# Attention over 16 images: one stream of steps across all batches, with the projections spread between them and every low part of the probabilities on GpSimd

## The chip, the core and the metric

The kernel runs on one core of one Trainium2 chip. TensorE (PE; its weight loads are the row PEld), VectorE (DVE), ScalarE (ACT) and GpSimd (POOL) compute, and SyncE (SP) issues the transfers. The metric is the device time of one execution in microseconds, as the median of several runs.

## What is computed

Each of 16 images is a batch of N = 1024 tokens with 512 channels, in float32, and goes through one attention layer of 8 heads of 64 dimensions:

```
qkv  = x @ w_qkv + b_qkv
qkv  = qkv.reshape(B, N, 8, 192)
q, k, v = jnp.split(qkv, 3, axis=-1)
attn = jnp.einsum('bxhd,byhd->bxyh', q, k) * 64 ** -0.5
attn = jax.nn.softmax(attn, axis=2)
res  = jnp.einsum('bxyh,byhd->bxhd', attn, v).reshape(B, N, 512)
out  = res @ w_out + b_out + x
```

## The kernel before

Float32 accuracy is kept with split operands. A number is the sum of a high part (rounded to fp32r, or to f16 for the probabilities P and for v) and a low part (what the rounding left), and a product is the sum of hi·hi, hi·lo and lo·hi. So a projection over 512 channels is 4 × 3 = 12 matmuls (`TERMS`), each with a 128 × 128 stationary operand and 512 moving columns.

**Fills.** Four kinds of work fill a PSUM bank for another engine to empty. `x_transpose` and `o_transpose` are four 128 × 128 transposes of a tile of 128 tokens (of x, or of the heads' output). `qk` (a head, half of the tokens), `v` (a tile of tokens, all heads) and `project` (a tile of tokens) are 12 matmuls each (line 472). ScalarE writes the high part (`xT_hi`, `v_parts`, `q_hi_hi`, `k_lo_hi`; lines 616 to 633), VectorE the low part (`xT_lo`, `v_parts`, `k_lo_hi`, `q_shift`; lines 712 to 728), and for `project` VectorE adds the sum to `y_tile` (line 736). SP copies q and k to the other 64 partitions once their high parts are there.

**Steps.** A unit is a head and half of its queries (16 units), and has 4 steps of 2 key tiles each, 64 steps a batch. TensorE computes the scores of a step (lines 532 and 534, two matmuls a tile), ScalarE takes the exponential of both tiles twice, as float32 `p_full` and as f16 `p_hi` (lines 654 and 655), VectorE or GpSimd subtracts them to get the low part `p_lo` (line 771 or 380, by `POOL_STEPS`), and TensorE multiplies with v in 24 small matmuls (lines 556 to 560, `step_pv`). The maximum of each row is found before: 8 matmuls a unit (line 503), each reduced by VectorE (line 749), joined, transposed (line 510) and put into `q_shift` (line 762), so that the scores come out with the maximum subtracted.

**Order.** Every engine has its program written out in order for one batch, and a loop over 16 batches runs it. A batch is a list `BEFORE` (8 x-transposes, the first 4 `v`, the first `qk`), then slots -5 to 65, then a list `AFTER`. In slot s TensorE issues the early row maxima, the scores of step s + 1, a piece of `qk` for the next head, the late row maxima, and P·V of step s - 1. The loop starts the next batch behind the last projection. PSUM has eight banks: four for scores, two in turn for row maxima, one for P·V, one for fills in the steps. Waits are on counting semaphores; TensorE and the other engines each take their instructions in order.

Of the kernel before, what the change touches and what calls it, by code (L numbers as in the profile page):

```python
# [19 lines left out]
Q_TILES = HALF // P  # L20
UNITS = HEADS * HALVES
STEPS_PER_UNIT = 4
STEPS = UNITS * STEPS_PER_UNIT
KEYS_PER_STEP = TOKENS // STEPS_PER_UNIT // P
X_SLOTS, Y_SLOTS, P_SLOTS = 4, 4, 3
SCORE_BANKS = (0, 1, 2, 3)
FILL_BANK_STEADY = 7
PV_BANK = 6
V_WIDTH = 2 * DIM + 2
PV_W = DIM + 1  # L30
FIRST_SLOT = -5
LAST_SLOT = STEPS + 1

MAX_TILES = (((0, 1), (2,)), ((3, 4), ()), ((5, 6), (7,)), ((), ()))
MAX_TILES_OF_UNIT = {0: (((0, 1), ()), ((2, 3), ()), ((4, 5), ()), ((6, 7), ())),
                     1: (((0, 1), ()), ((2, 3), ()), ((4, 5), (6,)), ((7,), ()))}


def max_tiles_of_slot(s, late=False):

    unit, slot = divmod(s + 5, STEPS_PER_UNIT)
    if not 0 <= unit < UNITS:  # L50
        return []
    tiles = MAX_TILES_OF_UNIT.get(unit, MAX_TILES)
    return [("row_max", unit, n // 2, n % 2) for n in tiles[slot][late]]


def shift_unit_of_slot(s):

    unit, rest = divmod(s + 2, Q_TILES)
    return unit if rest == 0 and 0 <= unit < UNITS else None


TERMS = 3 * CH_TILES


QK_PARTS = ({-5: (0, 1), -4: (1, 4), -3: (4, 8), -2: (8, TERMS)}, {0: (0, 6), 1: (6, TERMS)})
V_OF_SLOT = {-5: (4,), -4: (5,), -3: (6,), -2: (7,)}


def fills_of_slot(s):


    parts = [(("v", t), 0, TERMS) for t in V_OF_SLOT.get(s, ())]
    for h in range(1, HEADS):
        begin = 8 * (h - 1)
        for half in range(2):
            if s - begin in QK_PARTS[half]:
                parts.append((("qk", h, half), *QK_PARTS[half][s - begin]))
    tail = {STEPS - 2: (("o_transpose", 0), ("o_transpose", 1)),
            STEPS - 1: (("project", 0), ("o_transpose", 2)),
            STEPS: (("project", 1), ("o_transpose", 3), ("project", 2))}  # L80
    return parts + [(w, 0, TERMS) for w in tail.get(s, ())]


def completed_in_slot(s):

    return [w for w, _, last in fills_of_slot(s) if last == TERMS]


def is_first_half(w):
    return w[0] == "qk" and w[2] == 0  # L90


def consumed_in_slot(s):


    return ([w for w in completed_in_slot(s - 1) if is_first_half(w)]
            + [w for w in completed_in_slot(s) if not is_first_half(w)])


def high_parts_in_slot(s):  # L100


    parts = [(w, "k") for w in completed_in_slot(s - 1) if is_first_half(w)]
    for w in completed_in_slot(s):
        parts.append((w, "q" if is_first_half(w) else "qk"))
    return parts


def named(*names):

    kinds = {"T": ("x_transpose",), "V": ("v",), "Q": ("qk", 0)}
    return [(*kinds[name[0]], int(name[1])) for name in names]

BEFORE = named("T0", "T1", "T2", "T3", "V0", "T4", "T5", "Q0", "T6", "T7", "V1", "V2", "Q1", "V3")
AFTER = [("o_transpose", 4), ("project", 3), ("o_transpose", 5), ("project", 4), ("o_transpose", 6),
         ("project", 5), ("o_transpose", 7), ("project", 6), ("project", 7)]
SLOTS = range(FIRST_SLOT, LAST_SLOT + 1)

MAX_ORDER = []
for _s in SLOTS:
    MAX_ORDER += max_tiles_of_slot(_s) + max_tiles_of_slot(_s, late=True)
    if shift_unit_of_slot(_s) is not None:
        MAX_ORDER.append(("shift", shift_unit_of_slot(_s)))
MAX_AT = {w: n for n, w in enumerate(MAX_ORDER)}
MAXES = len(MAX_ORDER)

FILL_ORDER = BEFORE + [w for _s in SLOTS for w, _, last in fills_of_slot(_s) if last == TERMS] + AFTER
FILL_AT = {w: n for n, w in enumerate(FILL_ORDER)}  # L130
FILLS = len(FILL_ORDER)
assert FILL_ORDER == BEFORE + [w for _s in SLOTS for w in consumed_in_slot(_s)] + AFTER
HI_ORDER = [w for w in FILL_ORDER if w[0] != "project"]
HI_AT = {w: n for n, w in enumerate(HI_ORDER)}
HIS = len(HI_ORDER)


def fill_banks():


    banks, after = {}, 0
    for n, w in enumerate(FILL_ORDER):
# [12 lines left out]
FILL_BANK = fill_banks()


def last_in_bank(w):

    before = [u for u in FILL_ORDER[:FILL_AT[w]] if FILL_BANK[u] == FILL_BANK[w]]  # L160
    return before[-1] if before else None

POOL_STEPS = (0, 2, 3, 4, 6, 7)
LAST_UNIT_POOL_STEPS = (STEPS - 4, STEPS - 2)


def on_pool(s):  # L170
# [12 lines left out]

def signals(batch, per_batch, n):

    return batch * per_batch + n


def signals_led(batch, per_batch, n):

    return batch * per_batch + n + 1


def attention_block(nc: bass.Bass, x, w_qkv, b_qkv, w_out, b_out, out):
# [7 lines left out]
    with ExitStack() as ctx:  # L202
# [6 lines left out]

# [5 lines left out]
        xT_lo = sb("xT_lo", [P, CH_TILES, TOKENS], f32r)  # L215
        x_in = sb("x_in", [P, X_SLOTS, CH], f32)
# [7 lines left out]
        p_hi = sb("p_hi", [P, P_SLOTS, KEYS_PER_STEP, HALF], f16)  # L224
        p_lo = sb("p_lo", [P, P_SLOTS, KEYS_PER_STEP, HALF], f16)
# [15 lines left out]


# [593 lines left out]
```

## Time and profile before

| | |
|---|---|
| median of 3 runs | 4104.45 us (4103.89 to 4105.86) |
| the profiled execution | 4103.61 us, its span 4101.8 us |
| TensorE busy | 3915.1 us, 38156 matmuls |
| VectorE, ScalarE busy | 2721.0 us, 2707.0 us |
| GpSimd busy | 1769.3 us |
| granted TensorE clock | 1.00 of 2.4 GHz |

The span runs from the first to the last instruction. Matmuls overlap in the records, so TensorE's busy time says less than the distance from the start of one matmul to the start of the next.

### The profile page before, as it was taken

Reading aid. Unit: us, or ns where it says so; the run is one execution under the profiler, and the core shown is the slowest. Engines: PE = TensorE matmul, PEld = TensorE weight load, DVE = VectorE, ACT = ScalarE, POOL = GpSimd, SP = SyncE. Lnnn points to the kernel's source line nnn. Section 1 sums busy time; section 2 is a strip of 40 time slices with the busy share of each in tenths; the row PEclk is TensorE's granted clock in tenths of the full one; section 3 lists DMA queues with packets and bytes.
Section 4 is the critical chain, followed back from the end, with each engine's and each line's share of the span. In section 5 each row is a group of like instructions: output and inputs, shape, how many; then the busy total and the mean of one; then the engine's idle time right before and its main releaser. Section 6 shows DMA issues by size and latency. Waiting matters only on the chain.

```text
span 4101.8 us, 105442 instructions
## 1 busy us (share of the span) xinstructions
PE 3915.1 (95%) x38156; PEld 3113.8 (76%) x38156; DVE 2721.0 (66%) x4395; ACT 2707.0 (66%) x2965; POOL 1769.3 (43%) x888
## 2 busy tenths in 40 slices
PE   6999999999999999999999999999999999999999
PEld 5777777777777777777777777777777777777777
DVE  5757757577575775757667576675766757667576
ACT  4756847568475774757757477574775747657476
POOL 1534525345253552535525255352553525435254
PEclk9999999999999999999999999999999999999999
DMA  3011021110202102020021211202011121110201
GB/s 98 22 54 42 20 76 25 57 39 17 79 22 70 26 20 76 22 74 22 25 71 24 71 24 28 68 22 73 22 37 58 25 71 25 38 58 22 63 22 43
DMA packets 100845, 179.85 MB, mean 44 GB/s; under 512 B 16192, under 2 KB 16192, under 8 KB 100288
## 3 DMA queue, kind: packets, MB, share of 16 engines
q1 hardware_dynamic: 100288, 172.29, 14.9%
q8 instruction: 366, 6.00, 0.6%
q14 instruction: 191, 1.56, 0.1%
HBM read 71.57 MB, written 33.55 MB: 26 GB/s over the span
## 4 chain that ended last, share of the span: by engine, by line
PE 68%; DVE 17%; issue 11%; ACT 1%; DVEq 1%; POOL 1%; DMA 0%; SPq 0%; ACTq 0%; POOLq 0%
PE psum L472 31%; PE psum L503 9%; PE psum L532 6%; PE psum L534 6%; DVE max_parts L749 6%; PE psum L556 4%; PE psum L560 4%; PE psum L558 4%; DVE q_shift L728 3%; DVE k_lo_hi L726 3%; DVE p_lo L771 2%; PE psum L486 2%; DVE q_shift L762 2%; ACT p_hi L655 1%; POOL p_lo L380 1%
## 5 line engine op out<-in xcount | busy, mean ns | idle before, releaser
L380 POOL TENSOR_TENSOR p_lo<-p_full,p_hi 128x1024 f16<-128x1024 f32 x752 | 1607.3, 2143 | 2069.7 <-ACT p_hi L655 2069.7
L749 DVE TENSOR_REDUCE max_parts<-psum 128x1 f32<-128x512 f32 x2048 | 1341.3, 686 | 516.7 <-PE psum L503 507.8
L654 ACT ACTIVATE p_full<-psum,prob_bias 128x1024 f32<-128x1024 f32 x1024 | 1144.1, 1117 | 384.8 <-PE psum L534 371.1
L655 ACT ACTIVATE p_hi<-psum,prob_bias 128x1024 f16<-128x1024 f32 x1024 | 1137.2, 1111 | 0.0
L556 PEld LDWEIGHTS psum<-v_parts,p_hi 128*128 128x128 f16 x8192 | 743.8, 98 | 263.2 <-issue 161.8
L556 PE MATMUL psum<-v_parts,p_hi 128*128 128x65 f16 x8192 | 857.2, 193 | 35.5 <-DVE o_heads L781 19.9
L558 PE MATMUL psum<-v_parts,p_hi 128*128 128x64 f16 x8192 | 850.7, 192 | 0.0
L560 PE MATMUL psum<-v_parts,p_lo 128*128 128x65 f16 x8192 | 848.0, 194 | 0.0
L532 PE MATMUL psum<-q_hi_hi,k_lo_hi 128*128 128x512 f32 x2048 | 818.7, 400 | 1.9
L503 PE MATMUL psum<-k_lo_hi,q_hi_hi 128*128 128x512 f32 x2048 | 769.3, 429 | 51.7 <-DVE q_shift L728 21.5
L534 PE MATMUL psum<-q_shift,k_shift 128*128 128x512 f32 x2048 | 802.3, 392 | 0.0
L558 PEld LDWEIGHTS psum<-v_parts,p_hi 128*128 128x128 f16 x8192 | 753.9, 97 | 2.5
L560 PEld LDWEIGHTS psum<-v_parts,p_lo 128*128 128x128 f16 x8192 | 754.2, 97 | 0.0
L503 PEld LDWEIGHTS psum<-k_lo_hi,q_hi_hi 128*128 128x128 f32 x2048 | 367.3, 189 | 158.9 <-DVE q_shift L762 60.3
L534 PEld LDWEIGHTS psum<-q_shift,k_shift 128*128 128x128 f32 x2048 | 385.1, 188 | 73.4
L532 PEld LDWEIGHTS psum<-q_hi_hi,k_lo_hi 128*128 128x128 f32 x2048 | 385.0, 188 | 70.7 <-issue 3.8
L472 PE MATMUL psum<-xT_hi,wqkv_hi 128*128 128x512 f32 x1024 | 414.6, 405 | 11.6
L472 PE MATMUL psum<-xT_hi,wqkv_lo 128*128 128x512 f32 x1024 | 408.8, 399 | 0.0
L472 PE MATMUL psum<-xT_lo,wqkv_hi 128*128 128x512 f32 x1024 | 401.6, 392 | 0.0
L616 ACT CAST xT_hi<-psum 128x512 fp32r<-128x512 f32 x256 | 141.0, 593 | 367.3 <-PE psum L486 366.9
L625 ACT ACTIVATE q_hi_hi<-psum,qk_bias 64x512 fp32r<-64x512 f32 x256 | 174.3, 681 | 279.4 <-PE psum L472 279.4
L771 DVE TENSOR_TENSOR p_lo<-p_full,p_hi 128x1024 f16<-128x1024 f32 x272 | 332.2, 1221 | 31.1 <-ACT p_hi L655 31.1
(61 smaller groups left out, 4269.8 us busy)
## 6 DMA issues: line engine op xcount, KB each, us to landing
x_in<-in_x SPq DMA_DIRECT2D x128, 256.0 KB, 3.9
k_shift<-k_lo_hi SPq DMA_DIRECT2D x256, 128.0 KB, 2.2
q_hi_hi<-q_hi_hi SPq DMA_DIRECT2D x256, 128.0 KB, 2.3
y_tile<-in_x SPq DMA_DIRECT2D x128, 256.0 KB, 2.8
result<-y_tile SPq DMA_DIRECT2D x128, 256.0 KB, 2.8
o_heads<-in_L_conv_w_qkv SPq DMA_DIRECT2D x12, 256.0 KB, 4.1
o_heads<-in_L_conv_w_out SPq DMA_DIRECT2D x4, 256.0 KB, 4.1
out_bias<-in_L_conv_b_out SPq DMA_DIRECT2D x1, 256.0 KB, 5.8
```

Of the source, the lines that this page charges most:

```text
L380: nc.gpsimd.tensor_tensor(p_lo[:, s % P_SLOTS, :, :], p_full[:, s % 2, :, :], p_hi[:, s % P_SLOTS, :, :], ALU.subtract).then_inc(p_lo_read ...
L472: matmul = nc.tensor.matmul(fill_bank(w), a, b, start=n == 0, stop=n == TERMS - 1)
L503: nc.tensor.matmul(dst, q_hi_hi[:, h % 2, q0:q0 + P], k_lo_hi[:, h % 2, k_half * HALF:(k_half + 1) * HALF], start=True, stop=True).then_in ...
L532: nc.tensor.matmul(score_banks(s)[:, n, :], k_lo_hi[:, h % 2, keys], q_hi_hi[:, h % 2, cols], start=True, stop=False)
L534: last = nc.tensor.matmul(score_banks(s)[:, n, :], k_shift[:, h % 2, keys], q_shift[:, h % 2, cols], start=False, stop=True)
L556: nc.tensor.matmul(pv[:, qt, :], hi, v_parts[:, kt, h, DIM:DIM + PV_W], start=kt == 0 and qt == 0, stop=False, skip_group_check=True)
L558: nc.tensor.matmul(pv[:, qt, 0:DIM], hi, v_parts[:, kt, h, 0:DIM], start=False, stop=False, skip_group_check=True)
L560: last = nc.tensor.matmul(pv[:, qt, :], lo, v_parts[:, kt, h, DIM:DIM + PV_W], start=False, stop=kt == TOKEN_TILES - 1, skip_group_check=True)
L654: nc.scalar.activation(p_full[:, s % 2, :, :], score_banks(s), ACT.Exp, scale=SCALE, bias=prob_bias[:, :])
L655: nc.scalar.activation(p_hi[:, s % P_SLOTS, :, :], score_banks(s), ACT.Exp, scale=SCALE, bias=prob_bias[:, :]).then_inc(exp_done, 1)
L749: nc.vector.reduce_max(max_parts[:, u % 2, q_tile, k_half:k_half + 1], max_bank(w), AX.X).then_inc(max_tile_done, 1)
L771: nc.vector.tensor_tensor(p_lo[:, s % P_SLOTS, :, :], p_full[:, s % 2, :, :], p_hi[:, s % P_SLOTS, :, :], ALU.subtract).then_inc(p_lo_read ...
```

## The change

The loop's body is no longer a batch. All batches form one stream of steps, 64 a batch, and the fills of a batch are put at fixed slots relative to its step 0, from -17 to 103, so that they lie between steps of the batch before or after. Each engine's program is a first part (slots -17 to 45), a loop over 15 times 64 slots in which two batches meet, and a last part; SP's is written out whole. A table gives each fill its slot:

- x-transposes, the first half of `v` and the first `qk` stand in slots -17 to -1, that is in slots 47 to 63 of the batch before. `v` is now made in two groups of 4 heads, with 256 columns instead of 512, the second in slots 11 to 31.
- o-transposes stand in slots 62 to 72 and projections in 66 to 103, which are slots 2 to 39 of the next batch. They write to tiles of their own (`oT_hi`, `oT_lo`, 3 slots).
- In each slot TensorE does early row maxima, transposes, pieces of `qk`, `v` or `project`, scores, late row maxima, P·V. Slots 19, 27, 34, 42, 43 and 44 have no fill.
- Scores use three banks in turn (four before), and each of the two tiles of a step has its own signal and its own pair of exponentials of 512 columns (one pair of 1024 before). Two banks serve the fills, and two the row maxima.
- All of `p_lo` is made by GpSimd (6 of 8 steps before, 2 of 4 in the last unit). `p_hi` has 4 slots and `p_lo` 2 (3 each before); x tiles have 2 slots (4 before), y tiles 3 (4 before).
- Each kind of work has its own semaphores.

```diff
-STEPS_PER_UNIT = 4
-X_SLOTS, Y_SLOTS, P_SLOTS = 4, 4, 3
-SCORE_BANKS = (0, 1, 2, 3)
-FILL_BANK_STEADY = 7
...
+X_SLOTS, Y_SLOTS, O_SLOTS, HI_SLOTS, LO_SLOTS = 2, 3, 3, 4, 2
+V_GROUP = HEADS // 2
...
+SCORE_BANKS, PV_BANK, RING_BANKS, FILL_BANKS = (0, 1, 2), 6, (4, 5), (3, 7)
...
+FIRST_SLOT, LAST_SLOT = -17, STEPS + 39
+LOOP_SLOT = 46
+
+X_TRANSPOSE_SLOT = (-17, -16, -15, -13, -12, -12, -11, -10)
+O_TRANSPOSE_SLOT = (62, 64, 65, 67, 68, 69, 70, 72)
+PROJECT_PARTS = (((66, 0, TERMS),), ((67, 0, TERMS),), ((68, 0, TERMS),), ((69, 0, TERMS),), ((71, 0, TERMS),),
+                 ((74, 0, 6), (76, 6, TERMS)), ((99, 0, 6), (100, 6, TERMS)), ((103, 0, TERMS),))
+V_SLOT = ((-14, -13, -9, -6, -5, -4, -3, -1), (11, 15, 18, 20, 23, 26, 28, 31))
+Y_BIAS_SLOT = (54, 56, 58, 67, 69, 71, 73, 76)
...
+def qk_parts(h, half):
+
+
+    begin = 8 * (h - 1)
+    if half == 1:
+        return [(begin, 0, 6), (begin + 1, 6, TERMS)]
+    if h == 2:
+        return [(begin - 2, 0, TERMS)]
+    return [(begin - 3, 0, 4), (begin - 2, 4, TERMS)]
...
-POOL_STEPS = (0, 2, 3, 4, 6, 7)
-LAST_UNIT_POOL_STEPS = (STEPS - 4, STEPS - 2)
...
+POOL_STEPS = tuple(range(8))
...
+def slots(batches):
+
+    return {"first": [(c, (0,)) for c in range(FIRST_SLOT, LOOP_SLOT)],
+            "loop": [(c, (0, 1)) for c in range(LOOP_SLOT, LOOP_SLOT + STEPS)],
+            "last": [(c, (0,)) for c in range(LOOP_SLOT, LAST_SLOT + 3)]}[batches]
...
+            def exp_tile(i, g, n):
+                s = g % STEPS
+                if n == 0:
+                    if g >= 2 or not isinstance(i, int):
+                        wait_low(act, i, g - 2)
+                    wait_for(act, pv_done, i, STEPS, g + 1 - HI_SLOTS)
+                wait_for(act, scores_ready, i, SCORE_TILES, KEYS_PER_STEP * g + n + 1)
+                nc.scalar.activation(p_full[:, s % 2, n, :], scores(s, n), ACT.Exp, scale=SCALE, bias=prob_bias[:, :])
+                nc.scalar.activation(p_hi[:, s % HI_SLOTS, n, :], scores(s, n), ACT.Exp,
+                                     scale=SCALE, bias=prob_bias[:, :]).then_inc(exp_done, 1)
```

**VectorE, the end of a batch before,** as the instructions stand in its program: projections (`y_tile`) and o-transposes (`xT_lo`) follow each other with nothing between them.

```order
L736 TENSOR_TENSOR y_tile<-psum,y_tile 128x512 [waits y_biased]
L739 REGISTER_ALU
L710 REGISTER_ALU [waits fill_ready]
L712 TENSOR_TENSOR xT_lo<-psum,xT_hi 128x4x128 [waits hi_done]
L739 REGISTER_ALU
L734 REGISTER_ALU [waits fill_ready]
L736 TENSOR_TENSOR y_tile<-psum,y_tile 128x512 [waits y_biased]
```

**VectorE, the same work after the change,** in slots 2 and 3 of the next batch (`oT_lo` is the low part of an o-transpose):

```order
L746 TENSOR_REDUCE row_max<-max_parts 128x4 [waits row_max_done]
L726 SCALAR_TENSOR_TENSOR k_lo_hi<-psum,qk_bias,k_lo_hi 64x512 [waits qk_hi_done]
L728 SCALAR_TENSOR_TENSOR q_shift<-psum,qk_bias,q_hi_hi 64x512
L752 TENSOR_TENSOR q_shift<-psum,minus_block 4x512 [waits shift_ready]
L737 TENSOR_TENSOR y_tile<-psum,y_tile 128x512 [waits project_ready,y_biased]
L199 REGISTER_ALU
L742 TENSOR_REDUCE max_parts<-psum 128x1 [waits row_max_ready]
L199 REGISTER_ALU
L710 TENSOR_TENSOR oT_lo<-psum,oT_hi 128x512 [waits o_transpose_hi_done]
L199 REGISTER_ALU
L742 TENSOR_REDUCE max_parts<-psum 128x1 [waits row_max_ready]
L737 TENSOR_TENSOR y_tile<-psum,y_tile 128x512 [waits project_ready,y_biased]
```

The projection's addition now stands behind the low parts of q and k and the shift, and between row maxima.

**VectorE, a step in the middle of a head before,** with the low part of the probabilities between the output of a unit and a row maximum:

```order
L777 RECIPROCAL inv_sum<-psum 128x4 [waits pv_done]
L781 TENSOR_TENSOR o_heads<-psum,inv_sum 128x4x64 [waits inv_ready]
L769 REGISTER_ALU
L770 REGISTER_ALU [waits exp_done]
L771 TENSOR_TENSOR p_lo<-p_full,p_hi 128x1024 [waits pv_done]
L745 REGISTER_ALU
L749 TENSOR_REDUCE max_parts<-psum 128x1 [waits max_tile_ready]
```

After the change the row maximum follows the output directly; no p_lo is left in VectorE's program.

```order
L774 RECIPROCAL inv_sum<-psum 128x4 [waits o_ready,pv_done]
L777 TENSOR_TENSOR o_heads<-psum,inv_sum 128x4x64 [waits inv_ready]
L199 REGISTER_ALU
L742 TENSOR_REDUCE max_parts<-psum 128x1 [waits row_max_ready]
```

**TensorE after the change, slots 42 and 43,** which have no fill (line 504 is a row maximum, 512 the transpose for the shift, 536 and 538 scores, 558 the first of the 24 matmuls of P·V, left out here):

```order
L504 MATMUL psum<-k_lo_hi,q_hi_hi 128x512 [waits q_hi_hi_ready1,qk_done,row_max_done]
L536 MATMUL psum<-q_hi_hi,k_lo_hi 128x512 [waits exp_done]
L538 MATMUL psum<-q_shift,k_shift 128x512
L536 MATMUL psum<-q_hi_hi,k_lo_hi 128x512 [waits exp_done]
L538 MATMUL psum<-q_shift,k_shift 128x512
L199 REGISTER_ALU
L512 MATMUL psum<-identity,row_max 4x128 [waits max_joined,row_max_done]
L199 REGISTER_ALU [waits exp_done]
L558 MATMUL psum<-v_parts,p_hi 128x65 [waits p_lo_ready1]
...
L199 REGISTER_ALU [waits qk_done,row_max_done]
L504 MATMUL psum<-k_lo_hi,q_hi_hi 128x512 [waits q_hi_hi_ready0]
L536 MATMUL psum<-q_hi_hi,k_lo_hi 128x512 [waits exp_done,shift_done]
```

The first row maximum of slot 43 waits for the low parts of a `qk` that ended in slot 41, and the scores behind it for the shift of slot 42. Each of the two score tiles has a wait of its own; before, one wait stood ahead of both:

```order
L529 REGISTER_ALU
L532 MATMUL psum<-q_hi_hi,k_lo_hi 128x512 [waits exp_done]
L534 MATMUL psum<-q_shift,k_shift 128x512
L532 MATMUL psum<-q_hi_hi,k_lo_hi 128x512
L534 MATMUL psum<-q_shift,k_shift 128x512
```

## Rows read from the trace of the kernel before

**Rows 1.** The page: the span; busy time, share and instructions by engine.

```profile
span 4101.8 us, 105442 instructions
...
PE 3915.1 (95%) x38156; PEld 3113.8 (76%) x38156; DVE 2721.0 (66%) x4395; ACT 2707.0 (66%) x2965; POOL 1769.3 (43%) x888
```

**Rows 2.** The chain that ended last, in order of time: start, us, what.

```profile
1528.80 0.90 PE psum L486 x8
...
1545.86 2.77 PE psum L472 x12
...
1782.82 0.91 PE psum L486 x8
```

**Rows 3.** Timeline of TensorE, first transposes and last matmul: start, duration, instruction, [idle before].

```profile
35.06 1.96 PE L486 MATMUL psum<-identity,x_in 128*128 128x128 f32 x16 [0.50 <-DVEq L706]
...
4098.03 0.39 PE L472 MATMUL psum<-wout_hi,xT_lo 128*128 128x512 f32 x1
```

**Rows 4.** Timeline of TensorE, one P·V step of 24 and what follows.

```profile
1662.76 0.20 PE L556 MATMUL psum<-v_parts,p_hi 128*128 128x65 f16 x1
...
1663.50 0.71 PE L503 MATMUL psum<-k_lo_hi,q_hi_hi 128*128 128x512 f32 x2
1664.04 0.39 PE L472 MATMUL psum<-xT_lo,wqkv_hi 128*128 128x512 f32 x1
```

**Rows 5.** Groups by line and shape: xcount | busy, mean ns | idle before, releasers.

```profile
L380 POOL TENSOR_TENSOR p_lo<-p_full,p_hi 128x1024 f16<-128x1024 f32 x752 | 1607.3, 2143 | 2069.7 <-ACT p_hi L655 2069.7
L749 DVE TENSOR_REDUCE max_parts<-psum 128x1 f32<-128x512 f32 x2048 | 1341.3, 686 | 516.7 <-PE psum L503 507.8
...
L556 PE MATMUL psum<-v_parts,p_hi 128*128 128x65 f16 x8192 | 857.2, 193 | 35.5 <-DVE o_heads L781 19.9 <-POOL p_lo L380 15.7
...
L503 PE MATMUL psum<-k_lo_hi,q_hi_hi 128*128 128x512 f32 x2048 | 769.3, 429 | 51.7 <-DVE q_shift L728 21.5 <-DVE q_shift L762 11.9
...
L472 PE MATMUL psum<-xT_hi,wqkv_hi 128*128 128x512 f32 x1024 | 414.6, 405 | 11.6
...
L771 DVE TENSOR_TENSOR p_lo<-p_full,p_hi 128x1024 f16<-128x1024 f32 x272 | 332.2, 1221 | 31.1 <-ACT p_hi L655 31.1
...
L726 DVE SCALAR_TENSOR_TENSOR k_lo_hi<-psum,qk_bias,k_lo_hi 64x512 fp32r<-64x512 f32 x256 | 193.4, 755 | 98.7 <-ACT k_lo_hi L628 85.9 <-issue 6.1
...
L762 DVE TENSOR_TENSOR q_shift<-psum,minus_block 4x512 fp32r<-4x512 f32 x256 | 173.6, 678 | 144.1 <-PE psum L510 141.1
...
L616 ACT CAST xT_hi<-psum 128x512 fp32r<-128x512 f32 x256 | 141.0, 593 | 367.3 <-PE psum L486 366.9
```

**Rows 6.** Stretches, one head and one batch: busy (count) by engine, clock, DMA.

```profile
1648.80:1673.30 24.50, 24.09 (x268) 19.02 (x266) 18.29 (x31) 19.37 (x21) 13.29 (x7) 1.00 0.10 23
...
sum 254.00, PE 244.40 PEld 194.42 DVE 169.00 ACT 168.52 POOL 110.45; mean PE 27.16 PEld 21.60 DVE 18.78 ACT 18.72 POOL 12.27
```

**Rows 7.** Waits: who waited for whom, us in total, times, longest.

```profile
PEld psum L472 <- DVE q_shift L728: 59.6, 112, 0.6
...
PE psum L556 <- POOL p_lo L380: 15.7, 32, 0.6
```

**Rows 8.** Timeline of TensorE at the loop's jump, last projection and first transposes.

```profile
1557.37 0.39 PE L472 MATMUL psum<-wout_hi,xT_lo 128*128 128x512 f32 x1
1558.54 1.96 PE L486 MATMUL psum<-identity,x_in 128*128 128x128 f32 x16 [0.79 <-issue]
```

**Rows 9.** Timeline of TensorE, P·V of the last steps of a batch.

```profile
1779.58 0.20 PE L556 MATMUL psum<-v_parts,p_hi 128*128 128x65 f16 x1 [0.56 <-POOL p_lo L380]
...
1781.92 0.20 PE L556 MATMUL psum<-v_parts,p_hi 128*128 128x65 f16 x1 [0.42 <-POOL p_lo L380]
```

**Rows 10.** Timeline of ScalarE in the middle of a head.

```profile
1653.66 0.69 ACT L625 ACTIVATE q_hi_hi<-psum,qk_bias 64x512 fp32r<-64x512 f32 x1 [2.06 <-PE psum L472]
...
1655.07 1.11 ACT L654 ACTIVATE p_full<-psum,prob_bias 128x1024 f32<-128x1024 f32 x1
1656.08 1.10 ACT L655 ACTIVATE p_hi<-psum,prob_bias 128x1024 f16<-128x1024 f32 x1
```

**Rows 11.** DMA issues of the page: count, KB each, us from issue to landing.

```profile
result<-y_tile SPq DMA_DIRECT2D x128, 256.0 KB, 2.8
```

More of the change, by code:

```diff
@@ L43 @@
[L43 to L50, printed above, removed]
-        return []
[L52 to L59, printed above, removed]
@@ L62 @@
[L62 to L81, printed above, removed]
@@ L84, in completed_in_slot @@
[L84 to L106, printed above, removed]
@@ L109, in named @@
[L109 to L125, printed above, removed]
@@ L363, in _ @@
+            for t in range(TOKEN_TILES):
+                sp.wait_ge(y_stored[t], 16 * BATCH)
         @block.gpsimd
@@ new lines, in run @@
+            def run(i, part):
+                for g, rels in slots(part):
+                    if step_of(g, rels) is not None and on_pool(g):
+                        step_lo(i, g)
+                    for r in rels:
+                        for t in range(TOKEN_TILES):
+                            if Y_BIAS_SLOT[t] == g - STEPS * r:
+                                y_bias(i, r, t)
+            run(0, "first")
+            with pool.Fori(0, BATCH - 1) as i:
+                run(i, "loop")
+            run(BATCH - 1, "last")
@@ new lines, in fill @@
+            def fill(i, r, w, first, last):
+                if first == 0:
+                    claim(i, r, w)
+                    source = {"qk": ("x_transpose", 4 * w[-1] + 3), "v": ("x_transpose", w[-1]),
+                              "project": ("o_transpose", w[-1])}[w[0]]
+                    wait_work(pe, done, i, r, source)
+                width = V_GROUP * DIM if w[0] == "v" else HALF
+                for n, (a, b) in list(enumerate(terms_of(w)))[first:last]:
+                    matmul = nc.tensor.matmul(bank(w)[:, 0:width], a, b, start=n == 0, stop=n == TERMS - 1)
+                if last == TERMS:
+                    matmul.then_inc(ready[w[0]], 1)
@@ L590, in _ @@
+            run(0, "first")
+            with pe.Fori(0, BATCH - 1) as i:
+                run(i, "loop")
+            run(BATCH - 1, "last")
         @block.scalar
@@ L669, in _ @@
+            run(0, "first")
+            with act.Fori(0, BATCH - 1) as i:
+                run(i, "loop")
+            run(BATCH - 1, "last")
         @block.vector
@@ L818 @@
+            run(0, "first")
+            with dve.Fori(0, BATCH - 1) as i:
+                run(i, "loop")
+            run(BATCH - 1, "last")
 _INPUTS = ["x", "L0_conv_w_qkv", "L0_conv_b_qkv", "L0_conv_w_out", "L0_conv_b_out"]
```

829 lines of the change are left out of this document (418 added, 411 removed).

## The prediction

> **What bounds the kernel now.** I read the page first: TensorE is busy 95% of a span of 4101.8 us, VectorE and ScalarE 66%, GpSimd 43% [rows 1]. A busy share counts matmuls that merely overlap, so the next view is the chain of waits: one batch starts its transposes at 1528.80, the next at 1782.82, a period of 254.0 us [rows 2]. Sixteen of these are 4064; the first transpose starts at 35.06 and the last matmul at 4098.03, 3.7 before the end [rows 3], which gives 4103 in all. So one batch explains the kernel.
>
> How much of 254.0 is matmul work? The distance from start to start tells it, not the duration. Twelve 512-wide matmuls take 2.77, 0.231 each; eight transposes 0.90, 0.113 each [rows 2]. The 24 small matmuls of a P·V step start at 1662.76 and the next instruction at 1663.50, 0.0308 each; the pair of 512-wide ones behind them takes 0.54 where two should take 0.46, so 0.08 is lost on the way from small to wide, once a step [rows 4]. The counts of a batch are in the code, and those of the whole run bear them out (2048 for L503, 1024 for one of the forms of L472, 8192 for L556 [rows 5]): 768 wide ones, 1536 small ones, 80 transposes, 64 steps. So 768 × 0.231 = 177.4; 1536 × 0.0308 = 47.4; 80 × 0.113 = 9.0; 64 × 0.08 = 5.1; together **238.9**. The other **15.1 us a batch, 242 in all,** are TensorE standing still. By the stretches, a head in the middle takes 24.5 [rows 6]; its work is 72 × 0.231 + 192 × 0.0308 + 2 × 0.113 + 8 × 0.08 = 23.4, so some 1.1 is lost per head, 8 in seven heads, and the other 7 at the change of batch. What ends these stops: VectorE's q_shift (60 us ahead of L472's weight loads) [rows 7]; 0.79 of bare issue at the loop's jump [rows 8]; and in the last steps of a batch, which have no projection in them, GpSimd's p_lo, 0.56 and 0.42 [rows 9].
>
> **The change, part by part.**
> *One stream.* The opening of a batch (8 x-transposes, 8 v, the first qk) and its end (8 o-transposes, 8 projections) no longer stand alone: they lie between attention steps of the neighbouring batch. Their matmuls are the same, so the 238.9 stay; what goes is the stop. A slot of the new stream holds on average 239/64 = 3.7 us of TensorE work, against 3.06 in a head before (24.5/8). The others must fit under 3.7: ScalarE four half-tile exponentials a step, GpSimd one p_lo of 2.14, VectorE two reduces of 0.69 and a share of the rest [rows 5]. Per batch VectorE loses 17 p_lo of 1.22 and falls from 169.0 [rows 6] to about 148, and GpSimd rises to 64 × 2.143 = 137 and 8 small adds. Both are under 239.
>
> *Exponentials in halves.* No 512-wide exponential is in the trace. Consecutive 1024s start 1.0 apart, so 0.5 a half is the floor; q_hi and k_hi, 512 wide with a bias too, take 1.41 together, so 0.70 is the ceiling [rows 10]; the cast of 512 has 0.59 [rows 5], and I take 0.6: 2.4 a step instead of 2.0. ScalarE then has 64 × 2.4 + 16 × 1.4 + 32 casts of at most 0.59 = 195 a batch, hidden under 239, but not in every slot.
>
> *v in two groups.* 96 wide matmuls become 192 of 256 columns. Rows bound one at 0.113 (a transpose of 128 columns) and 0.231 (512). Half of 0.231 is 0.116; a transpose's weights load within its 0.113, so a load fits under 0.116, and I take 0.119: 192 × 0.119 − 96 × 0.231 = +0.7 a batch. At the ceiling it is +22.2, on the straight line between the two rows (0.152) +7.0. The Trainium skill (TensorE: Matmul & The Clock Gate, Back-to-back issue gap) gives N/2.4 + 2.5 ns for a warm matmul, 0.109 for 256; by that, an estimate, the term would be −1.2. The trace has 0.231 where the same formula says 0.216.
>
> *All low parts on GpSimd.* 272 of them go from 1.22 on VectorE to 2.14 [rows 5], 0.92 more from exponential to P·V in 17 steps a batch. That is hidden if TensorE has other work: P·V of a step follows its scores by more than one whole slot, 0.23 + 0.74 + 3.7 + about 2 = 6.7, and must wait for two half tiles (2.4), sometimes q_hi and k_hi (1.4), and p_lo (2.14 and some 0.3 of signals): 4.9 or 6.3. With a fill in the slots it fits. Without one it does not: before, two steps without a fill follow each other at 1779.58 and 1781.92, 2.34 apart, for 1.74 of work [rows 9].
>
> *What stays as waiting,* worked out from the table of slots. (a) The loop's jump, 1.0 a batch [rows 8]. (b) Slots 42 and 34 have no fill: qk of the next head ends at t in the slot before; the first half tile is through at t + 1.9, q_hi and k_hi (1.4) at 3.3, VectorE's k_lo and q_shift (0.75 each) at 4.9. TensorE is at the first row maximum that reads them at t + 4.05 (0.92 + 0.23 + 0.82 and a slot of 2.08): 0.85 of waiting in each; in 42 the scores behind it then wait for the shift (0.68 on VectorE), 0.45 more. Together 2.15. (c) Slots 19, 27, 43 and 44, without a fill, at 2.34 instead of 2.2: with margin 0.2 each, 0.8. (d) Slots 3 to 6, each with 12 wide matmuls and a transpose: the project_add that frees a PSUM bank comes last on VectorE, 0.2 late each, 0.8. Sum **4.8 a batch**, against 15.1.
>
> *Waits added.* Scores now wait for exp_done per tile, with three banks in place of four: the tile three back must be through. That is 5.5 us of stream for a chain of about 2, so nothing. SP waits in order for y stores (2.8 us to land [rows 11]) ahead of q and k copies; those are read some five slots later, so nothing. GpSimd's y_bias waits for such a load with p_lo queued behind it; P·V stands some 5 us later there, as slots 2 to 7 are the longest. If that cover fails, it is 1 to 2 us a batch.
>
> *Once.* The first steps of batch 0 and the last 17 of batch 15 lack the neighbour's work, some 25 slots × 0.2 = 5; the opening with two x buffers instead of four, 6; the end, 2: 13, all estimates from (c) and from the 15.1.
>
> *Sum.* 16 × (238.9 + 0.7 + 4.8) = 3910.4; + 35.1 + 3.7 + 13 = 3962 for the span. The profiled execution takes 1.8 us more than its span (4103.6 against 4101.8), and the median of the runs, 4104.45, is 0.8 above that: **3964**, 3.4% less.
>
> **Rivals.**
> *GpSimd sets the step (the other side).* If every one of the 17 steps a batch shows its 0.92: 250 us, 4214. It decides once p_lo adds 9 us a batch, 0.52 in each of the 17. For it: both waits of [rows 9] name GpSimd, and 2.14 is 1.75 times 1.22. Against: TensorE's whole wait on p_lo is 15.7 us in 32 places [rows 7], though GpSimd has three steps in four. Beside it stands the Trainium skill (GPSIMD Engine Reference, Engine selection), which sends elementwise work to VectorE, as GpSimd is about twice as slow on two inputs; the trace agrees roughly on the ratio, and by that rule taken alone the change loses.
> *The waits only move.* In order, with two fill banks and two for the maxima, the 15.1 may all come back: 3964 + 16 × 10.3 = 4129. Against: the wait for q_shift ahead of L472 came from one fill bank, and VectorE is freed of p_lo.
> *ScalarE is late.* With halves at 0.70 a step is 2.8, and six short slots and the two of (b) grow by 0.45 each: 3.6 a batch, 4022.
> *Narrow matmuls cost more.* At 0.152: 6.3 a batch more, 4065; at 0.231: 21.5 more, 4308.
> *Nothing but the jump is left:* 3.8 a batch less, 3903.
>
> **How the numbers follow.** Forecast 0.62 (its own range 3920 to 4010), ScalarE late 0.12, narrow matmuls at 0.152 0.07, nothing but the jump 0.08; at 0.231 0.01, GpSimd 0.06, waits only move 0.04. Below 3880 lies about 0.05 and above 4070 about 0.13, so the range is 3880 to 4070. A run tells about 0.2% (8 us) from no change. Faster is the sum of the first four, 0.89; half of "waits only move" is the same, 0.02; the rest slower, 0.09.
>
> **What would show it.** A period near 244 in place of 254; TensorE's waits for q_shift and at the change of batch gone, but for some 1 us at the jump and the first row maxima of two heads; exponentials starting 0.5 to 0.7 apart; v's matmuls 0.11 to 0.13 apart; P·V waiting for p_lo in steps without a fill alone. It is wrong if P·V waits for p_lo in most steps, if v's matmuls are 0.15 or more apart, or if the wait for a fill bank or a row-maximum bank is the largest on TensorE.

## The result and the profile after

The changed kernel takes 4081.73 us (median of 4 runs, 4078.49 to 4086.39) beside 4104.97 (4103.89 to 4105.86) for the kernel before on the same chip: a ratio of 0.9944, interval 0.9927 to 0.9962. It is faster, but by 0.6%, where 3.4% was forecast. The profiled execution took 4083.68 us. Its page, to be laid beside [rows 1]:

```profile
span 4081.9 us, 108064 instructions
PE 3912.5 (96%) x39692; PEld 3225.1 (79%) x39692; DVE 2456.8 (60%) x4251; ACT 3040.0 (74%) x5141; POOL 2355.5 (58%) x1160
...
q8 instruction: 364, 5.96, 0.6%
```

VectorE became lighter and ScalarE and GpSimd heavier, as forecast, and TensorE is as busy as it was. So TensorE still bounds the kernel, and the question is where it stands still. The waits of TensorE in the changed kernel, in the columns of [rows 7]:

```profile
PE psum L504 <- issue: 54.3, 19, 4.8
PE psum L429 <- DVE k_lo_hi L697: 30.2, 1, 30.2
PE psum L504 <- DVE q_shift L728: 20.7, 31, 1.6
PE psum L494 <- DVE q_shift L728: 19.3, 15, 1.3
PE psum L494 <- DMA x_in<-in_x: 8.0, 13, 2.4
...
PE psum L558 <- POOL p_lo L399: 2.8, 5, 1.2
```

The second row is the start, alike in both kernels. P·V's wait for GpSimd is nearly gone (2.8 us after 15.7 [rows 7]). At the change of batch waits are left ahead of the x-transposes (L494), 19.3 and 8.0 us. On top stands a wait for nothing: "issue", in front of a row maximum (L504), up to 4.8 us long. It is at the jump of TensorE's loop, at the end of slot 45. The timeline of TensorE there, changed kernel, the last P·V matmul and what follows:

```profile
1729.71 0.20 PE L562 MATMUL psum<-v_parts,p_lo 128*128 128x65 f16 x1
1733.17 0.49 PE L504 MATMUL psum<-k_lo_hi,q_hi_hi 128*128 128x512 f32 x1 [3.27 <-issue]
1733.50 0.54 PE L479 MATMUL psum<-xT_lo,wqkv_hi 128*128 128x512 f32 x1
1733.84 0.63 PE L479 MATMUL psum<-xT_hi,wqkv_lo 128*128 128x512 f32 x1
1734.27 0.63 PE L479 MATMUL psum<-xT_hi,wqkv_hi 128*128 128x512 f32 x1
```

TensorE stands still for 3.3 us, and soon behind it the same 512-wide matmuls start 0.43 apart instead of 0.23. Three stretches around the jump at 1478.62 show why (us, then busy time and count of PE, PEld, DVE, ACT, POOL, then the granted clock; the last two columns are the DMA's):

```profile
1477.57:1481.00 3.43, 1.25 (x27) 0.86 (x25) 0.76 (x2) 1.91 (x4) 1.76 (x1) 1.00 0.05 12
1481.00:1487.83 6.83, 5.49 (x13) 4.25 (x14) 0.85 (x2) 1.02 (x3) 2.13 (x1) 0.50 0.01 4
1487.83:1494.66 6.83, 5.54 (x70) 4.46 (x69) 4.95 (x8) 5.75 (x11) 1.61 (x1) 1.00 0.25 57
```

The clock is at 0.50 (1.2 GHz) in a stretch that begins in the stop, and back at 1.00 (2.4 GHz) behind it. So it is after each of the 14 jumps; the kernel before had 1.00 at its jumps. The mean granted clock is 0.989 for the whole run.

The trace also holds a record for the branch itself, the instruction that sends TensorE back to the start of its loop; the views leave it out. When TensorE jumps back, that record lasts 3.36 to 5.04 us in the changed kernel and 4.04 to 5.01 us in the kernel before; at the last turn, where it does not jump, 0.08; on ScalarE, VectorE and GpSimd 0.04 to 0.06, always. In the kernel before the branch executes 3.5 us ahead of the start of the last matmul, with 16 wide matmuls still to run, and in the changed kernel 0.39 us ahead, with 14 small ones.

### The profile page after: what moved, and what is told of

The parts are those of the page before. It is cut to its first block, busy times and chain, and to the rows that moved or that the text cites. A ratio compares the mean times of both kernels' runs of the same rounds, so it can differ in the third digit from the quotient of the medians.

```text
span 4081.9 us, 108064 instructions
## 1 busy us (share of the span) xinstructions
PE 3912.5 (96%) x39692; PEld 3225.1 (79%) x39692; DVE 2456.8 (60%) x4251; ACT 3040.0 (74%) x5141; POOL 2355.5 (58%) x1160
## 4 chain that ended last, share of the span: by engine, by line
PE 90%; issue 3%; DVE 3%; ACT 2%; DMA 2%; POOL 0%; SPq 0%; DVEq 0%; ACTq 0%; POOLq 0%
PE psum L479 35%; PE psum L504 13%; PE psum L536 11%; PE psum L538 11%; PE psum L558 6%; PE psum L562 6%; PE psum L560 5%; PE psum L494 3%; DMA x_in<-in_x 1%; DVE q_shift L728 1%; ACT p_hi L642 1%; DVE max_parts L742 1%; ACT k_lo_hi L624 1%; PE psum L512 1%; ACT q_hi_hi L622 1%
## 5 line engine op out<-in xcount | busy, mean ns | idle before, releaser
L399 POOL TENSOR_TENSOR p_lo<-p_full,p_hi 128x1024 f16<-128x1024 f32 x1024 | 2194.6, 2143 | 1684.2 <-ACT p_hi L642 1641.6
L742 DVE TENSOR_REDUCE max_parts<-psum 128x1 f32<-128x512 f32 x2048 | 1388.2, 689 | 1135.8 <-PE psum L504 1116.7
L641 ACT ACTIVATE p_full<-psum,prob_bias 128x512 f32<-128x512 f32 x2048 | 1423.5, 695 | 685.4 <-PE psum L538 660.4
L642 ACT ACTIVATE p_hi<-psum,prob_bias 128x512 f16<-128x512 f32 x2048 | 1417.8, 692 | 18.7 <-issue 18.7
L504 PE MATMUL psum<-k_lo_hi,q_hi_hi 128*128 128x512 f32 x2048 | 853.1, 437 | 76.0 <-issue 54.3
L504 PEld LDWEIGHTS psum<-k_lo_hi,q_hi_hi 128*128 128x128 f32 x2048 | 387.3, 190 | 124.5 <-issue 79.1
L479 PE MATMUL psum<-xT_lo,wqkv_hi 128*128 128x512 f32 x1024 | 413.6, 404 | 0.0
L752 DVE TENSOR_TENSOR q_shift<-psum,minus_block 4x512 fp32r<-4x512 f32 x256 | 173.8, 679 | 298.7 <-PE psum L512 294.9
L479 PE MATMUL psum<-wqkv_hi,xT_hi 128*128 128x256 f32 x1024 | 290.6, 284 | 1.9 <-DVE xT_lo L710 1.4
L479 PE MATMUL psum<-wqkv_hi,xT_lo 128*128 128x256 f32 x1024 | 290.0, 283 | 0.0
```

Of the source, the lines that this page charges most:

```text
L399: nc.gpsimd.tensor_tensor(p_lo[:, g % LO_SLOTS, :, :], p_full[:, g % 2, :, :], p_hi[:, g % HI_SLOTS, :, :], ALU.subtract).then_inc(p_lo_re ...
L479: matmul = nc.tensor.matmul(bank(w)[:, 0:width], a, b, start=n == 0, stop=n == TERMS - 1)
L504: nc.tensor.matmul(bank(w), q_hi_hi[:, h % 2, q0:q0 + P], k_lo_hi[:, h % 2, k_half * HALF:(k_half + 1) * HALF], start=True, stop=True).the ...
L641: nc.scalar.activation(p_full[:, s % 2, n, :], scores(s, n), ACT.Exp, scale=SCALE, bias=prob_bias[:, :])
L642: nc.scalar.activation(p_hi[:, s % HI_SLOTS, n, :], scores(s, n), ACT.Exp, scale=SCALE, bias=prob_bias[:, :]).then_inc(exp_done, 1)
L742: nc.vector.reduce_max(max_parts[:, u % 2, q_tile, k_half:k_half + 1], bank(w), AX.X).then_inc(done["row_max"], 1)
```

## Experiments

**Theory A:** a jump costs TensorE's instruction supply some 4 us in both kernels; what is queued behind the branch hides it, 3.5 us of wide matmuls before and 0.4 us of small ones now; the stop lowers the clock, which costs some 2 us more. **Rival B:** TensorE waits there for the other engines, which jump in the same slots, or for their data. **Rival C:** the missing gain was eaten by GpSimd's longer low parts.

**Another place for the cut.** The loop's jump is moved from the end of a slot into slot 46; no instruction changes its place in the order. `ahead` is the first half of a slot (early row maxima, transposes, fills, scores), `behind` the second (late row maxima, shift, P·V).

```
 def run(i, part):
     for n, (g, rels) in enumerate(slots(part)):
         if part == "first" or n > 0:
             ahead(i, g, rels)
         behind(i, g, rels)
+    if part != "last":
+        ahead(i, g + 1, rels)
```

> TensorE's instructions and their order stay as in the changed kernel; only the place of its loop's jump moves, from the end of slot 45 (behind 24 small P·V matmuls) to the middle of slot 46 (behind 8 wide projection matmuls and 4 wide score matmuls). Theory A (a jump takes a fixed 4.1 to 4.7 us from the branch to the next matmul, and only what is still queued behind the branch hides it; the clock falls because TensorE then stands still): 12 wide matmuls hide about 2.8 us, so the stop falls from about 3.7 to 1.0-1.6 us, the granted clock stays at 1.00 behind it, and the time falls by 14 x (2.4 to 4.8) = 35 to 67 us, to 4015-4047. Rival B (TensorE stops there because the other engines jump in the same slot, so that its data are late): the stop stays in slot 45/46 or follows the other engines, 4074-4090.

Measured: 4052.11 us (ratio to the kernel before 0.9874, 0.9858 to 0.9889), 30 us better than the changed kernel and just outside what theory A gave. The stop shrank less than it said: matmuls start 2.4 to 3.3 us apart at the jump, and in 11 of 14 the clock still falls. The records show why: only 4 to 6 matmuls were left when the branch executed, 0.75 to 1.20 us, since the score matmuls wait for exponentials and the branch comes behind that wait.

**A longer cover.**

```
-    if h == 2:
+    if h in (2, 7):
         return [(begin - 2, 0, TERMS)]
```

> As the run before it, and the first q and k projection of head 7 is taken whole in slot 46 (12 wide matmuls in place of 4 in slot 45 and 8 in slot 46), so that 16 wide matmuls stand ahead of the jump. Theory A: about 3.6 us are hidden, the stop is 0.5 to 1.1 us, the clock does not fall, 4005-4035, at or below the run with 12. Rival B: 4074-4090.

Measured: 4046.89 us (0.9858, 0.9843 to 0.9873); not to be told from the run before, and again above what was expected. In part the reason is the same: 4 to 9 matmuls behind the branch, 0.68 to 2.00 us, starts 1.9 to 3.3 apart. Now the clock falls in 7 of 14. The other part is that P·V now waits 11.4 us for o_heads, 1.6 in the run before.

**The projection directly ahead of the jump.**

```
+at_jump = g % STEPS == LOOP_SLOT
+if at_jump and step_of(g + 1, rels) is not None:
+    step_scores(i, g + 1)
 for r in rels:
     for piece in fills_of_slot(g - STEPS * r):
         fill(i, r, *piece)
-if step_of(g + 1, rels) is not None:
+if not at_jump and step_of(g + 1, rels) is not None:
     step_scores(i, g + 1)
```

> As the cut behind 16 wide matmuls, but in that one slot the four score matmuls, which wait for exponentials, come first and the twelve of the projection stand directly ahead of the jump, so that nothing keeps the branch from running ahead of them. Theory A (3.6 to 4.3 us from the branch to the next matmul; hidden is what is queued behind the branch when it executes): 12 to 16 wide matmuls are queued, 2.5 to 3.5 us, so starts lie 0.7 to 1.6 us apart at the jump, the granted clock stays at 1.00 there, 4010-4032. Rival D (the jump's stop cannot be hidden further than in the two cuts before, because TensorE waits for something else there): starts 2 to 3 us apart as in those, 4040-4055.

Measured: 4046.19 us (0.9855, 0.984 to 0.987). At the jump it is as theory A has it: 12 or 13 matmuls behind the branch, 2.74 to 2.84 us, starts 0.76 to 1.34 apart, and the clock stays at 1.00 at all 14 jumps. But the time missed the range, because the scores, now early in their slot, stand where their PSUM bank is not yet read. The timeline of TensorE in this kernel, at the scores and then at the jump:

```profile
2465.84 0.50 PE L536 MATMUL psum<-q_hi_hi,k_lo_hi 128*128 128x512 f32 x1 [1.18 <-ACT p_hi L654]
...
2468.92 0.39 PE L479 MATMUL psum<-xT_hi,wqkv_lo 128*128 128x512 f32 x1
2469.81 0.27 PE L512 MATMUL psum<-identity,row_max 128*4 128x128 f32 x1 [0.50 <-issue]
```

1.18 us moved to the exponential, 0.50 is left at the jump. In the whole run the scores wait 21.5 us for the exponential, 5.9 in the changed kernel, and P·V 11.4 for o_heads, 1.6 there; without these 25 us the time would be some 4021, an estimate, inside theory A's range. Rival D's range holds the time, but the starts are not the 2 to 3 us apart that it needs.

**Fewer jumps.** TensorE's loop takes five batches a turn, and in another run none: all 16 are written out. The other engines keep their loops.

```
+turn = ([(c, tuple(range(TURN + 1))) for c in range(LOOP_SLOT, LOOP_SLOT + STEPS * TURN)]
+        if part == "loop" else slots(part))
-with pe.Fori(0, BATCH - 1) as i:
+with pe.Fori(0, BATCH - 1, TURN) as i:
```

and for none

```
+turn = [(c, tuple(range(BATCH))) for c in range(FIRST_SLOT, STEPS * (BATCH - 1) + LAST_SLOT + 3)]
-run(0, "first")
-with pe.Fori(0, BATCH - 1) as i:
-    run(i, "loop")
-run(BATCH - 1, "last")
+run(0, "all")
```

> TensorE's loop takes five batches in a turn (2 jumps back in place of 14), the jump left where it is; all other engines keep one batch a turn. Theory A: 12 of 14 stops and their clock falls go, 12 x 5.5 to 6.5 us: 4000-4020; the two jumps left look as before. Rival B (other engines' jumps, or instructions that come late wherever the program goes on): the stops stay at the old period of 251 us, or come back inside the longer turn, 4070-4090.

> The changed kernel with TensorE's 16 batches written out and nothing else changed. Theory A: 14 jumps of the changed kernel cost (4082 - 4016) / 12 = 5.5 us each, so without any the time is 4016 - 2 x 5.5 = 4005 (3998-4012), against 4111 of the kernel before without a jump. Rival B': a longer program costs by itself, as it may have in the kernel before (4111 against 4103): 4012-4025.

Measured: 4015.74 us with two jumps (0.9788, 0.9775 to 0.9801) and 4004.36 without (0.9753, 0.974 to 0.9766). The first gives (4081.73 − 4015.74) / 12 = 5.5 us a jump, and from that 4005 was forecast for the second. Of TensorE's waits in the kernel without a jump, the row in which the changed kernel has 54.3 us and up to 4.8 at a time:

```profile
PE psum L504 <- issue: 17.4, 35, 0.8
```

Rival B falls: the other engines still jump in every batch, and no stop of the old period is left. Rival B', that a longer program costs by itself, gave 4012 to 4025 and falls for this stream. Written out, TensorE also has some 2800 instructions less, of registers above all; as the second time came out where the jumps alone put it, these cost nothing that shows.

**The split of the low parts undone.** `POOL_STEPS = (0, 2, 3, 4, 6, 7)`: VectorE takes two of eight again.

> Only the split of the low parts is undone: GpSimd takes six steps of eight, VectorE the other two (before it had 47 of 64 on GpSimd). Theory A (the low parts are hidden, the missing gain lies at the jump): 4074-4090, no difference to be measured. Rival C (the missing gain was eaten by GpSimd's longer low parts): 10 us or more faster than the changed kernel, below 4070.

Measured: 4087.93 us (0.9963, 0.9949 to 0.9976), beside 0.9927 to 0.9962 for the changed kernel. The two can't be told apart, and rival C falls: VectorE's part brings nothing back.

**The same place in the kernel before.** If the cover is what counts, the old stream must suffer from a bad cut as the new one does.

```
+CUT = 31
-for s in SLOTS:
+for s in [s for s in SLOTS if (head if s < CUT else tail)]:
...
-with pe.Fori(0, BATCH) as i:
+batch((0, 0), True, False)
+with pe.Fori(0, BATCH - 1) as i:
+    batch((i, 0), False, True)
+    batch((i, 1), True, False)
+batch((BATCH - 1, 0), False, True)
```

> The kernel before, with TensorE's instructions in their old order, but the cut of its loop moved from the end of a batch (behind 12 wide projection matmuls) into the middle of it, behind the 24 small P·V matmuls of slot 30; the other engines' loops stay as they are. Theory A (3.6 to 4.3 us from branch to next matmul, hidden by what is queued): the visible stop grows from 1.3 to 3.3-3.7 us, the granted clock falls behind it as in the changed kernel (2.1 us more), so the kernel before becomes slower by 15 x 3.5 to 4.5 us, to 4150-4172. Rival B'' (the long stop belongs to the new stream, not to the place of the cut): 4100-4115 and a granted clock of 1.00.

Measured: 4171.13 us, slower by 1.66% (1.0166, 1.0152 to 1.018), inside theory A's range. The timeline of TensorE in this kernel shows the stop of the changed one:

```profile
2241.46 0.19 PE L564 MATMUL psum<-v_parts,p_lo 128*128 128x65 f16 x1
2244.92 1.22 PE L507 MATMUL psum<-k_lo_hi,q_hi_hi 128*128 128x512 f32 x2 [3.27 <-issue]
```

The clock falls behind 13 of its 14 jumps. The jumps of the six kernels with one batch a turn, from the records of the branch and of the matmuls (us). The first column of times runs from the branch to the start of the last matmul that was queued behind it, the second from there to the start of the next matmul, the third is their sum; the last counts the jumps behind which the granted clock fell to 0.50:

```
kernel                  branch to last start   starts apart   branch to next   clock falls
changed                 0.39-0.40              3.32-4.99      3.72-5.39        14 of 14
before, cut behind P·V  0.37-0.40              3.32-3.84      3.71-4.24        13 of 14
cut behind scores       0.75-1.20              2.40-3.29      3.57-4.25        11 of 14
cut, 16 wide            0.68-2.00              1.89-3.33      3.58-4.08         7 of 14
fill ahead of the jump  2.74-2.84              0.76-1.34      3.57-4.16         0 of 14
before                  3.50-3.54              0.81-1.76      4.35-5.27         0 of 15
```

The third column stays near 4 us while the first goes from 0.4 to 2.8; in the kernel before, with 3.5, it is 4.9 in the mean. That is theory A, but for the higher price in the kernel before, to which the run with four loops comes back.

**The kernel before without a jump.**

> The kernel before with TensorE's 16 batches written out, no jump. Theory A: the 1.3 us that were visible at 15 jumps go, 4082-4090. Against it stands the new stream without a jump: what the change is worth apart from the jump is the difference of the two. Rival B': a longer program costs something by itself, 4100 or more.

Measured: 4111.35 us, not faster but slower by 0.2% (1.002, 1.0011 to 1.0029): theory A missed. The timeline of TensorE at the change of batch, first what follows [rows 8] in the kernel before and then this one:

```profile
1561.73 0.50 PE L472 MATMUL psum<-wqkv_hi,xT_hi 128*128 128x512 f32 x1 [1.23 <-DVE xT_lo L712]
```

```profile
1560.80 0.60 PE L488 MATMUL psum<-identity,x_in 128*128 128x128 f32 x4
1561.84 1.53 PE L488 MATMUL psum<-identity,x_in 128*128 128x128 f32 x12 [0.44 <-DVE y_tile L740]
1565.01 0.47 PE L474 MATMUL psum<-wqkv_hi,xT_hi 128*128 128x512 f32 x1 [1.64 <-DVE xT_lo L716]
```

Without the jump TensorE waits for y_tile and longer for xT_lo instead; from the last projection matmul to the first 12-matmul fill of the next batch it takes 4.34 to 4.59 us with the jump and 4.41 to 4.71 without. So the jump of the kernel before was not hidden by the 16 matmuls alone: what they left visible stood beside another wait, and it cost nothing. Why this kernel is 8 us slower was not found; some 0.1 a batch of it lies at the change of batch. Rival B' gave its time, 4100 or more, but it did not hold for the new stream, which came at 4004.36 written out. Without a jump in either, the change is worth 4111.35 − 4004.36 = 107 us, 2.6%.

**What the jump's price hangs on.** Ahead of the changed kernel TensorE runs four loops of four turns, whose results nothing reads.

```
+for body in (1, 200, 600, 1200):
+    with pe.Fori(0, 4):
+        for _ in range(body):
+            nc.tensor.transpose(psum[:, FILL_BANKS[0], 0:P], identity[:, :], identity[:, :])
```

> A measurement of the jump by itself: ahead of the changed kernel TensorE runs four loops of four turns, with 1, 200, 600 and 1200 transposes of the identity in the body (some 0.11 us each, 900 us in all, whose results are not used), so the time of this run tells nothing of the change. The branch's own record on TensorE lasts 3.4 to 5.0 us when it jumps back over a whole batch. If the jump has one price whatever it jumps over (theory A in its plain form), all 12 jumps back of the four loops have records of 3 to 5 us. If the price is that of fetching a body that is too long to be kept, the short bodies (1 and 200) have records under 0.2 us and the long ones 3 to 5 us.

Measured: the branch's record lasts 0.21 to 0.24 us over a body of 1, 200 or 600 transposes (under 0.2 was expected of the short ones), and 3.64, 3.41 and 3.29 us over 1200. The timeline of TensorE shows the same, first across a jump of the loop of 600 (at 156.87), then behind two jumps of the loop of 1200:

```profile
90.81 131.38 PE L427 MATMUL psum<-identity 128*128 128x128 f32 x1202
...
488.06 131.22 PE L427 MATMUL psum<-identity 128*128 128x128 f32 x1200 [1.69 <-issue]
620.75 131.22 PE L427 MATMUL psum<-identity 128*128 128x128 f32 x1200 [1.47 <-issue]
```

1202 transposes run on without a gap across a jump over 600; each jump over 1200 leaves 1.3 to 1.7 us visible, behind 16 queued transposes of 0.11. So theory A's one price for every jump falls: a jump costs 3.3 to 5.0 us only when the body is long. A transpose has a weight load and a matmul, so 600 are 1200 instructions and 1200 are 2400; a batch of the changed kernel has some 2 × 2480. What the price is for can be seen on queue q8, which carries TensorE's instructions: in the kernel without a jump its 328 packets of 16 KB stand against 84026 instructions of TensorE, 256 each. The DMA of this run, first over the last three turns of the loop of 600 (156.8 to 353 us), then over one turn of the loop of 1200 (617.3 to 749.9):

```profile
DMA packets 0, 0.00 MB, mean 0 GB/s; under 512 B 0, under 2 KB 0, under 8 KB 0
```

```profile
q8 instruction: 11, 0.18, 0.6%
```

The body of 1200 instructions is not loaded again; the body of 2400, 9.4 packets long, is loaded anew in every turn. In the ten runs with a jump over a long body there are 120 such jumps. In each, a packet of q8 starts 0.8 to 1.6 us after the branch, and the branch's record ends 1.3 to 1.8 us after that packet does (2.1 in two cases). So TensorE waits for its next instructions. In the kernel before this packet takes 1.6 to 2.2 us, in its variant with the cut behind P·V 0.9 to 1.4; the difference, 0.8 in the mean, is most of the 0.9 by which the table has the price of the kernel before higher. The Trainium skill (Advanced Engine Details and Errata, ISA Cache) gives TensorE 128 KB of instruction cache in lines of 16 KB, 256 instructions each. An estimate from these figures is 2048 in all; the measurement agrees, since 1200 stay and 2400 do not. The same page of the Trainium skill (Control Flow Timing) has some 108 ns for a compare-and-branch; that is near the 0.08 of a branch not taken, half of the 0.21 over a short body, and 30 to 50 times too little for a jump over a batch.

**The x-transpose's bank.** One row of the waits of the changed kernel, 19.3 us ahead of L494, is the second x-transpose of a batch, which takes the bank of head 7's first projection. It goes into the bank of the first transpose, with five batches a turn, then without a jump, then with the projection behind it moved one slot later as well.

```
-FILL_BANKS[0] if w == ("project", 6) else min(FILL_BANKS, key=lambda k: free[k])
+FILL_BANKS[0] if w == ("project", 6) else of[b, ("x_transpose", 0)] if w == ("x_transpose", 1)
+else min(FILL_BANKS, key=lambda k: free[k])
```

> Five batches a turn on TensorE, and the second x-transpose of a batch goes into the PSUM bank of the first instead of the bank of head 7's projection. The stop of 1.53 us ahead of that transpose, once a batch, named VectorE's q_shift. Theory: the bank of the first transpose is free by then, so 15 x 1.5 = 23 us go: 3988-4000. Rival: the transpose then waits for the first transpose's low part, or the projection behind it does: the time stays at 4010-4020.

> TensorE has no loop at all (all 16 batches written out), and the bank of the run before it. Theory A: the two stops left with five batches a turn go too, 2 x 5.5 us, 11 us below that run: 3977-3989, a period of 243.7 us and the rest at the opening and at the end of the stream. Rival B' (a longer program makes its instructions arrive late): stops of bare issue at other places, no faster than five batches a turn.

> The stream without a jump and with the bank of the first x-transpose, and head 7's second projection taken whole one slot later, since it now waits 1.0 us for the bank that the transpose left. Theory (that wait is the whole of what the move of the bank left): 15 x 1.0 us less, 3980-3985. Rival: the first row maximum behind it then waits for its q and k, and nothing is won: 3993-4000.

Measured: 4018.67 us (0.9788, 0.9775 to 0.9802), 3997.27 (0.9741, 0.9727 to 0.9754) and 4011.89 (0.9775, 0.9762 to 0.9788). All three lie above what was expected. With five batches a turn nothing is won; without a jump the median is 7 us lower where 23 were expected, and the intervals overlap; with the projection moved it is 15 us higher again. Most of the stop goes to the next fill of that bank; TensorE in the second kernel:

```profile
1463.88 0.60 PE L495 MATMUL psum<-identity,x_in 128*128 128x128 f32 x4
1465.32 0.50 PE L480 MATMUL psum<-xT_hi,wqkv_hi 128*128 128x512 f32 x1 [0.84 <-DVE q_shift L727]
```

And when that fill is moved, the slot becomes too short for ScalarE, and the scores wait, 21.5 us in all where the second kernel has 6.1; TensorE in the third:

```profile
1470.05 0.50 PE L537 MATMUL psum<-q_hi_hi,k_lo_hi 128*128 128x512 f32 x1 [0.58 <-ACT p_hi L641]
...
1471.21 0.50 PE L537 MATMUL psum<-q_hi_hi,k_lo_hi 128*128 128x512 f32 x1 [0.42 <-ACT p_hi L641]
```

By its median the fastest kernel of the study is the one without a jump and with the other bank, 2.6% under the kernel before.

## Why the prediction was wrong

**The step that failed is term (a), "The loop's jump, 1.0 a batch [rows 8]".** The 0.79 was the part of a branch of some 4.6 us that 16 wide matmuls had left visible, taken over to a place where 0.4 us is queued. There TensorE is idle for 3.7 us in the mean, and the clock falls, for which the sum had no term at all: 77.4 us for 14 jumps (4081.73 − 4004.36), 5.5 each, where the forecast had 1.0. Nor was it a cost in the kernel before, as the run without it shows. The price was to be had, in the trace though not in its views: the branch's record in the trace of before lasts over 4 us.

**The ledger of a batch holds otherwise.** The second x-transpose of two batches in the kernel without a jump, in the timeline of TensorE:

```profile
2202.55 0.66 PE L494 MATMUL psum<-identity,x_in 128*128 128x128 f32 x4 [1.28 <-DVE q_shift L726]
...
2447.58 0.66 PE L494 MATMUL psum<-identity,x_in 128*128 128x128 f32 x4 [1.29 <-DVE q_shift L726]
```

They are 245.0 apart; over 14 batches the period is 245.3. Forecast without the jump was 239.6 of work and 3.8 of waiting, 243.4. The work was right: in 48 of the 64 slots the starts agree with the forecast's prices within 0.06. The other slots hold the waits: 1.5 a batch for the bank of that transpose, which the forecast had left out although the order of the fills shows it; 2.4 in slots 34, 35, 42 and 43, term (b), where 2.15 was worked out; 0.5 for terms (c) and (d), where 1.6 was; and 1.5 in slots 46, 62 and 63, for which the forecast had nothing. v's 256-wide matmuls (forecast 0.119) and the exponentials in halves (forecast 0.6) in the timelines of TensorE and ScalarE in the changed kernel:

```profile
1506.55 0.28 PE L479 MATMUL psum<-wqkv_hi,xT_hi 128*128 128x256 f32 x1
1506.67 0.28 PE L479 MATMUL psum<-wqkv_lo,xT_hi 128*128 128x256 f32 x1
1506.79 0.28 PE L479 MATMUL psum<-wqkv_hi,xT_lo 128*128 128x256 f32 x1
```

```profile
1606.13 0.68 ACT L642 ACTIVATE p_hi<-psum,prob_bias 128x512 f16<-128x512 f32 x1
1606.70 0.69 ACT L641 ACTIVATE p_full<-psum,prob_bias 128x512 f32<-128x512 f32 x1
1607.28 0.70 ACT L642 ACTIVATE p_hi<-psum,prob_bias 128x512 f16<-128x512 f32 x1
```

They start 0.12 and 0.57 apart. The formula of the Trainium skill for the gap of a single matmul (TensorE: Matmul & The Clock Gate, Back-to-back issue gap), 0.109 for 256 columns, is a little short here too.

**"Once" was too small.** In the kernel without a jump the span of 4002.5 less 16 × 245.3 is 77.7; less the 35.1 and 3.7 of the two ends, 39 are left, where 13 was forecast. In its opening TensorE waits for x and for the first transposes:

```profile
40.03 0.63 PE L494 MATMUL psum<-identity,x_in 128*128 128x128 f32 x4 [2.31 <-DMA x_in<-in_x]
42.06 0.58 PE L479 MATMUL psum<-wqkv_hi,xT_hi 128*128 128x256 f32 x1 [1.40 <-DVE xT_lo L708]
```

Together: 77.4 − 16 at the jump, 16 × 1.9 = 30 in the batches, 26 once: 118, and the span is 4081.9 where 3962 was worked out, 120 more.

**The rivals.** GpSimd does not set the step, although every low part takes 2143 ns there: P·V waits 2.8 us for them in all, and the run with the split undone is no faster. The rule of the Trainium skill that sends elementwise work to VectorE (GPSIMD Engine Reference, Engine selection) does not decide here, as GpSimd has the slack (58% busy). Nearest in size was "Narrow matmuls cost more" at 0.152, 4065, but not in mechanism: those matmuls start 0.12 apart. "The waits only move", 4129, is wrong too: of 15.1 us of waiting a batch 5.7 were left, and a cost that the old order had covered came out. "ScalarE is late" needed exponentials 0.70 apart, and they start 0.57 apart; "Nothing but the jump is left" falls by the same 5.7. None of the three signs of being wrong came: P·V does not wait for p_lo in most steps, v's matmuls are not 0.15 apart, and the largest wait on TensorE is not for a bank. A larger wait at the jump was not among the signs.

## What to carry to other kernels

Before a loop's cut is moved, read the branch's own record on the engine that sets the time: it gives the price of the jump, and the visible stop beside it is only what the queue left. For a long body put the cut behind long matmuls that wait for nothing, or take more batches into a turn; in these kernels a short stop also spared the clock. An idle time ascribed to one cause is a cost only if no second wait stands beside it: take it away and see.

## What was not expected of the hardware

A jump on TensorE cost 0.21 us over 1200 instructions and 3.3 to 3.6 over 2400; where between the two the step lies was not measured. Behind the 60 jumps that follow small P·V matmuls, in six runs, starts 3.3 to 5.0 us apart, the granted clock fell to 0.50 in 56 cases; in the two kernels with 0.8 to 1.8 it fell in none of 29, and between in some. What the lowered clock costs is, by an estimate, the rest of the 5.5 a jump: 3.8 is the stop (starts 3.9 apart in the mean, less 0.1), which leaves 1.7.
